# Gated attention and feed-forward block: query path by tokens with DMA turns, matrix integers on GpSimd, one set of loads for three head groups

## The chip, the cores and the metric

One core of one Trainium2 chip. The metric is the time of the whole kernel on the device in microseconds (us), smaller being better; three runs before gave 962.68 to 965.32 us, median 962.88.

## What is computed

Activations x of shape (4, 512, 512) in float32 go through four gated residual steps; the context is (4, 512, 512). The changed part lies between the second and the third.

```python
x = x + tanh(g_xattn[0]) * wkv(w, u, layernorm(x), ctx)       # a recurrence over 512 positions
n = layernorm(x)
h = silu(bitlinear(n, w1)) * bitlinear(n, w2)                 # activations to 8 bits by groups of 64
x = x + tanh(g_ffn[0]) * bitlinear(h, w3)                     # weights are signs times a mean
n = layernorm(x)
q = qdq(n) @ qdq(wq).T + bq      # qdq: scale of a row = max|.| / 127, round, clip to 127
k, v = split(ctx @ wkv.T + bkv)
o = softmax(q k^T / sqrt(32)) v                               # 16 heads of 32
x = x + tanh(g_xattn[1]) * (qdq(o) @ qdq(wp).T + bp)
x = x + tanh(g_ffn[1]) * (quantised rmsnorm(x) @ ternary(W).T)
```

## The kernel before

The program is written engine by engine: SyncE (all DMAs), GpSimd, ScalarE, TensorE and VectorE each have one list of instructions in order, and semaphores join them. Nothing is planned by a tool; the order on each engine is the order of the code. X, all 2048 tokens, stays in SBUF as 16 token tiles of 128.

**Stages.** Set-up and recurrence end at about 191 us. Then comes the feed-forward stage, one token tile after another (i = 0 to 15), each in four slots (j = 0 to 3) of 512 hidden columns. In a slot TensorE makes the two up products of tile i (`up`, line 1098: 16 matmuls, halves of fp16 high and low parts) and the down product of tile i - 1 (`down`, line 1110: 8 matmuls). VectorE takes the pair to a quantised hidden block: `hidden` (lines 1516 to 1521), after ScalarE's rounding `scaled` (1527). ScalarE writes the fp16 high part (811), GpSimd the low part (594), and SyncE turns the block by a DMA transpose (`turn_h`, 419). `up` of slot c waits until `scaled` of slot c - 2 is done. Between these lie the preparation of the tile to come (`prep_...`; 1425 to 1436) and two passengers:

- the **query path**, a few tiles behind: statistics (1540), normalising (831), maximum and scale (1548 to 1550), rounding (835), integers (1555). Then `q_turn` (1119, 1121) turns the integers on TensorE, and multiplies ones by a diagonal matrix of the token scales, which GpSimd made (606), to have them along columns; ScalarE copies both out (841, 842); `q_project` (1132) makes 16 matmuls of 128 columns, the result with channels on the partitions; VectorE multiplies the scales in (`q_full`, 1560), ScalarE applies channel scale and bias in four pieces (848) and the high part (852), GpSimd the low part (612). All queries stand in `QALL`, channels on partitions.
- the **matrices** wq, W and wp: for each VectorE takes row maxima (1568), ScalarE rounds (818), VectorE makes the integers (1587; 1589 and 1590 for the ternary one), SyncE turns four blocks (461). `matrix_work` (lines 328 to 331) says in which slot: maxima in tiles 1 and 7, integers one slot late from tiles 2, 5 and 8; the mean of W at tile 4 (1578).

**Seam.** After the last up part SyncE loads keys, values and queries of batch 0 from DRAM and `QALL` into `KS`, `VB` and `QS`, which lie where the up weights lay: for each of four head groups 3 + 1 + 12 DMAs (426, 429, 438), two groups, then the offsets, then the two others. TensorE meanwhile finishes the last down parts and query tiles 12 to 15; `first_rows` are the score rows of group 0.

**Attention.** 16 groups (4 batches of 4 head groups), 16 slots each. In a slot TensorE makes about one score row for the group to come (`rows`, 1161), whose maximum VectorE takes (1642), and a score tile of this group (`scores`, 1180), ScalarE its exponential (936); `weigh` (1190) multiplies with the values. GpSimd adds the weights, eight additions a group (`add_weights`, 663). The maxima are turned (`c_turn`, 1169), split into a high part (909) and a low part (1650) and sent as two rows into `QS` (`send_c`, 447); the first `scores` of a group waits for them. Then comes the output stage.

Of the kernel before, what the change touches and what calls it, by code (L numbers as in the profile page):

```python
# [5 lines left out]
F32 = mybir.dt.float32  # L6
# [54 lines left out]
def flamingo_kernel(nc, x, ctx_2048, g_xattn, g_ffn, w, u, w1, w2, w3, wq, bq, wkv, bkv, wp, bp, gamma, wl, out):  # L61
    stack = ExitStack()
    with stack:
# [29 lines left out]
        W_, U_, BQ, BK = vec[:, 0:4], vec[:, 4:8], vec[:, 8:12], vec[:, 12:16]  # L93
# [4 lines left out]
        vrows = sb("vrows", [4 * DB, P], F32)  # L98
# [67 lines left out]
        at = used[0]  # L166

# [6 lines left out]
        SXB, DIAG = part(P, F32), part(P, F32)  # L174
        QF, QB = part(D, F32, "p (k t) -> p k t", k=DB), part(D, F32, "p (k t) -> p k t", k=DB)
# [4 lines left out]
        wm_ints = B[:, used[0]:used[0] + DB * D].rearrange("p (k d) -> p k d", k=DB)  # L180
        OT, SM = part(512, F32), part(512, F32)
# [18 lines left out]
        swp_dram = nc.dram_tensor("swp_row", (D,), F32, kind="Internal").ap()  # L200
# [42 lines left out]
        st3, rstd3, qs3, rnd3, li3, diag3 = sem("st3"), sem("rstd3"), sem("qs3"), sem("rnd3"), sem("li3"), sem("diag3")  # L243
        lt_out, sx_ps, qp_ps, qb_ready = sem("lt_out"), sem("sx_ps"), sem("qp_ps"), sem("qb_ready")
# [15 lines left out]
        NSMALL = 6  # L260
# [76 lines left out]
        def _(sp):  # L337
            for to, frm in ((vrows[0:4, :], by_block(w)), (vrows[4:8, :], by_block(u)), (vrows[8:12, :], by_block(bq)),
                            (vrows[12:16, :], by_block(bkv[0:D])),
                            (TG[:, 0:2], on_all(g_xattn, 2)), (TG[:, 2:4], on_all(g_ffn, 2))):  # L340
                sp.dma_start(to, frm).then_inc(small_in, 16)
# [90 lines left out]
            def load_q(b, g):  # L432
                if g == 0:
                    sp.wait_ge(q_hi, b * TB + TB)
                    sp.wait_ge(q_lo, b * TB + TB)
# [22 lines left out]
            def turn_block(m, k):  # L458

                sp.wait_ge(wm_ready, DB * m + k + 1)  # L460
                sp.dma_start_transpose((WQT, WLT, WPT)[m][:, :, k * P:k * P + P], wm_ints[:, k, :]).then_inc(wm_out, 16)

            load_matrix(0)
            sp.wait_ge(ff_scales, 1)
            for i in range(TOK):
                for j in range(FC):
                    turn_h(i, j)
                    for m, k in matrix_work(i, j, INTS):
                        turn_block(m, k)
                        if k == DB - 1 and m < 2:  # L470
                            load_matrix(m + 1)
                    if (i, j) == (INTS[2] + 1, 1):
                        sp.dma_start(swp_dram.rearrange("(k p) -> p k", p=P), SWQP[:, 4:8],
                                     allow_slow_non_contiguous=True).then_inc(swp_io, 16)
                    if (i, j) == (INTS[2] + 3, 1):
                        sp.wait_ge(swp_io, 16)
# [1335 lines left out]
```

## Time and profile before

| | us |
|---|---|
| median of three runs | 962.88 (962.68 to 965.32) |
| profiled execution, its own time | 966.35 |
| its span from first to last instruction | 964.6 |
| TensorE busy | 821.9 |
| VectorE busy | 759.5 |
| ScalarE busy | 576.9 |
| GpSimd busy | 487.2 |
| set-up and recurrence | 0 to 191 |
| feed-forward stage, up parts | 191 to 555 |
| seam | 555 to 594 |
| attention | 594 to 864 |
| output stage | 864 to 965 |

PE is TensorE (PEld its weight loads), DVE VectorE, ACT ScalarE, POOL GpSimd, SPq SyncE's queue. Matmuls overlap, so their start-to-start distance is the time that they hold the engine; a row for several shows the time from the first start to the last end. Starts are in us from the start of the span. In brackets stands the idle time before, and what ended it. Spans on GpSimd are rough.

### The profile page before, as it was taken

The page shows a single profiled execution, that of the slowest core. Times are in us where ns is not written, and L with a number is a line of the kernel's source. Part 1 is how long each engine was busy: PE and PEld are TensorE (multiplying, and loading weights), DVE is VectorE, ACT ScalarE, POOL GpSimd, SP SyncE. Part 2 cuts the span into 40 slices and gives each one's busy share as a digit, 9 for nine tenths or more (in the row PEclk, how much of TensorE's full clock was granted, in tenths as well). Part 3 has the DMA queues.
Part 4 walks back from the last instruction along what each step waited for, and adds up shares of the span by engine and source line. Part 5 has one row for each costly group of instructions (what it writes and reads, how often), then busy time and mean ns, then how long its engine had stood idle before and what let it go on. Part 6 is the DMA issues. An engine that isn't in the chain of part 4 may idle for free.

```text
span 964.6 us, 14534 instructions
## 1 busy us (share of the span) xinstructions
PE 821.9 (85%) x4373; PEld 353.2 (37%) x4373; DVE 759.5 (79%) x1510; ACT 576.9 (60%) x974; POOL 487.2 (51%) x560
## 2 busy tenths in 40 slices
PE   2899987789898989899999968799999999974754
PEld 2544443334344444444444432222223232222321
DVE  4699998879899899999998758477777777634884
ACT  3588886543555565666665544466666666655762
POOL 2866663223334444444444343475757575764761
PEclk9999999899999999999999986899999999996886
DMA  8668875533353442352433241212122221000111
GB/s 283 214 178 221 223 204 151 143 88 65 62 115 55 72 103 57 63 70 55 79 65 65 45 100 54 84 49 79 55 77 57 72 61 46 1 1 0 43 66 66
DMA packets 172392, 86.51 MB, mean 90 GB/s; under 512 B 124048, under 2 KB 156960, under 8 KB 172320
## 3 DMA queue, kind: packets, MB, share of 16 engines
q1 hardware_dynamic: 172320, 85.64, 35.6%
q8 instruction: 34, 0.56, 0.2%
q14 instruction: 38, 0.31, 0.1%
HBM read 37.76 MB, written 12.58 MB: 52 GB/s over the span
## 4 chain that ended last, share of the span: by engine, by line
PE 37%; DVE 22%; issue 7%; ACT 6%; SPq 4%; DMA 3%; POOL 0%; ACTq 0%; DVEq 0%
PE bank L1098 10%; PE bank L1190 5%; PE bank L1161 5%; PE bank L1110 4%; PE bank L1180 4%; DMA A<-B 3%; DVE bank L1516 3%; DVE gsm L1518 3%; DVE B L1527 2%; SPq L438 2%; DVE B L1521 2%; PE bank L1307 2%; ACT bank L806 2%; PE bank L1209 2%; PE bank L1199 2%
## 5 line engine op out<-in xcount | busy, mean ns | idle before, releaser
L1098 PE MATMUL bank<-A,B 128*128 128x512 f16 x1024 | 233.0, 381 | 15.8 <-DVE B L1527 15.6
L1642 DVE TENSOR_REDUCE B<-bank 128x1 f32<-128x512 f32 x256 | 168.0, 683 | 73.9 <-PE bank L1161 73.9
L936 ACT ACTIVATE A<-bank 128x512 f32<-128x512 f32 x256 | 144.1, 593 | 106.9 <-PE bank L1180 103.5
L594 POOL TENSOR_TENSOR B<-B 128x512 f16<-128x512 f32 x64 | 76.4, 1193 | 223.4 <-DVE B L1527 147.2
L1098 PEld LDWEIGHTS bank<-A,B 128*128 128x128 f16 x1024 | 98.8, 98 | 142.9 <-DVE B L1527 20.6
L663 POOL TENSOR_TENSOR B<-A 128x512 f32<-128x512 f32 x64 | 79.3, 1269 | 96.0 <-ACT A L936 96.0
L806 ACT ACTIVATE bank<-B 128x512 f32<-128x512 f32 x64 | 38.5, 602 | 137.4 <-DVE B L1521 137.4
L1110 PE MATMUL bank<-A,B 128*128 128x512 f16 x512 | 120.7, 379 | 0.0
L1180 PE MATMUL bank<-A 98*128 98x512 f16 x256 | 94.5, 390 | 21.2 <-ACT A L936 10.5
L1161 PE MATMUL bank<-A 96*128 96x512 f16 x256 | 97.7, 409 | 7.9 <-DMA A<-B 4.7
L663 POOL TENSOR_TENSOR B<-B,A 128x512 f32<-128x512 f32 x64 | 79.0, 1264 | 0.1
L1190 PE MATMUL bank<-A,B 128*32 128x512 f32 x512 | 69.6, 616 | 1.0 <-ACT A L936 1.0
L1110 PEld LDWEIGHTS bank<-A,B 128*128 128x128 f16 x512 | 49.5, 98 | 54.3 <-DMA B<-B 0.4
L1073 PE MATMUL bank<-B 128*128 128x512 f16 x192 | 47.2, 399 | 17.9 <-DVE B L1411 17.9
L1527 DVE SCALAR_TENSOR_TENSOR B<-bank,gsm 128x512 f32<-128x512 f32 x64 | 44.2, 691 | 16.1 <-ACT bank L806 14.0
L1516 DVE SCALAR_TENSOR_TENSOR bank<-bank,ffs,B 128x512 f32<-128x512 f32 x64 | 48.2, 753 | 9.1 <-PE bank L1098 8.6
L1161 PEld LDWEIGHTS bank<-A 96*128 96x128 f16 x256 | 23.3, 100 | 85.0 <-DVE B L1642 65.3
L801 ACT ACTIVATE B<-bank,ffs 128x512 f32<-128x512 f32 x64 | 43.1, 673 | 13.4 <-PE bank L1098 13.1
L549 POOL TENSOR_SCALAR B<-X,mv,rs 128x128 f32<-128x128 f32 x64 | 49.8, 792 | 0.4
L1180 PEld LDWEIGHTS bank<-A 98*128 98x128 f16 x256 | 25.0, 99 | 67.2 <-ACT A L936 36.6
L1062 PE MATMUL bank<-B 128*128 128x512 f16 x192 | 46.1, 392 | 0.0
L1518 DVE TENSOR_REDUCE gsm<-bank 128x8 f32<-128x512 f32 x64 | 44.3, 692 | 2.2
(216 smaller groups left out, 1479.5 us busy)
## 6 DMA issues: line engine op xcount, KB each, us to landing
B<-in_L_ffn_w_dram SPq DMA_DIRECT2D x48, 256.0 KB, 3.4
A<-k_parts SPq DMA_DIRECT2D x48, 128.0 KB, 2.6
A<-B SPq DMA_DIRECT2D x192, 32.0 KB, 1.9
X<-in_x_dram SPq DMA_DIRECT2D x4, 1024.0 KB, 9.4
B<-in_ctx_dram SPq DMA_DIRECT2D x16, 256.0 KB, 4.4
k_parts<-B SPq DMA_DIRECT2D x16, 256.0 KB, 4.3
v_rows<-B SPq DMA_DIRECT2D x16, 256.0 KB, 2.3
B<-v_rows SPq DMA_DIRECT2D x16, 256.0 KB, 3.4
```

The costliest lines, as they stand in the source:

```text
L594: nc.gpsimd.tensor_tensor(HLb[j][:, 1, :], Db[j % 2], HLb[j][:, 0, :], ALU.subtract).then_inc(lo_done, 1)
L663: nc.gpsimd.tensor_tensor(ACC[j], PR[j] if t == 1 else ACC[j], PR[(HG * t + j) % 8], ALU.add).then_inc(acc_done, 1)
L936: nc.scalar.activation(PR[(HG * t + j) % 8], bank[2 + j % 2][:, :], ACT.Exp, scale=SCALE).then_inc(exp_done, 1)
L1098: last = mm(bank[2 * n + q][:, :], XQT[a][:, m, :], wt[:, m % DB, j * 512:j * 512 + 512], start=(m == 0), stop=(m == 2 * DB - 1))
L1110: last = mm(bank[5 + q][:, :], HT[j][:, m, :], W3T[:, DB * j + m % DB, :], start=(j == 0 and m == 0), stop=(j == FC - 1 and m == 2 * DB - 1))
L1161: mm(bank[ROW_BANKS[r % 3]][:, :], QS[0:96, HG * g + j, t * P:t * P + P], KS[0:96, HG * g + j, :], start=True, stop=True).then_inc(row_ps, 1)
L1180: mm(bank[2 + j % 2][:, :], KS[0:98, HG * g + j, t * P:t * P + P], QS[0:98, HG * g + j, :], start=True, stop=True).then_inc(st_ps, 1)
L1190: last_ = mm(bank[6][DH * j:DH * j + DH, :], VB[:, t, (HG * g + j) * DH:(HG * g + j + 1) * DH], PR[(HG * t + j) % 8], start=(t == 0), stop ...
L1516: stt(H, H, C2, SAb[q], ALU.mult, ALU.mult).then_inc(h_done, 1)
L1518: link(reduce(gsm[:, 0, :], grouped(H), AX.X, ALU.max, apply_absolute_value=True))
L1527: stt(grouped(Db[q]), grouped(bank[q][:, :]), RND, spread(1), ALU.subtract, ALU.mult).then_inc(d_done, 1)
L1642: reduce(NMX[g % 2][:, t, j:j + 1], bank[ROW_BANKS[r % 3]][:, :], AX.X, ALU.max, negate=True).then_inc(row_max, 1)
```

## The change

- Query integers are turned by a DMA transpose (`turn_ints`); `q_turn` and the diagonal matrix go. `q_project` makes four matmuls of 512 columns with tokens on the partitions, one slot earlier. ScalarE scales out of PSUM by token (`q_scale`), GpSimd multiplies the channel scales and adds the bias (`q_affine`, two operations of full width), ScalarE and GpSimd make the two parts, and a second DMA transpose puts them into `QALL` (`turn_q`). `q_full` and `q_bias` go.
- The matrices' integers are made on GpSimd, in two buffers.
- The mean of W is taken at the second slot of tile 4, not at its last.
- One scale of the activation groups reads 1024 from a per-partition operand instead of an immediate.
- Channel scales of wq and wp go through DRAM to a row on all partitions; the query bias is loaded over the value bias.
- At the seam group 0 is loaded alone, the other three groups by one set of 3 + 1 + 12 larger DMAs. Query tiles 13 to 15 are finished during the score rows and inside attention; the last one's turn stands ahead of the offsets of group 2.

```diff
@@ SyncE
+            def turn_ints(u):
+                sp.wait_ge(li3, u + 1)
+                up_to(sp, qp_ps, u)
+                sp.dma_start_transpose(LT, LI).then_inc(lt_in, 16)
+
+            def turn_q(u):
+                sp.wait_ge(q_hi, u + 1)
+                sp.wait_ge(q_lo, u + 1)
+                sp.dma_start_transpose(QALL[:, :, :, u * P:u * P + P].rearrange("p h k s -> p (h k) s"),
+                                       QHL[u % 2].rearrange("p h d -> p (h d)")).then_inc(qT_in[u % 2], 16)
...
+                    if j == 0 and i > 4:
+                        turn_q(i - 5)
+                    if j == 1 and i > 2:
+                        turn_ints(i - 3)
...
-            for g in range(2):
-                load_kv(0, g, True)
-                load_q(0, g)
+            def load_others():
+                for slot, part_ in ((0, 0), (1, 0), (2, 1)):
+                    ins = sp.dma_start(KS[DH * slot:DH * slot + DH, HG:HEADS, :],
+                                       k_dram[0][part_, P:D, :].rearrange("(j p) s -> p j s", p=DH))
+                    ins.then_inc(kv_in[1], 16)
+                sp.dma_start(VB[:, :, P:D], v_dram[0].rearrange("(t p) d -> p t d", p=P)[:, :, P:D]).then_inc(kv_in[1], 16)
+                for slot, part_ in ((0, 0), (1, 1), (2, 0)):
+                    for j in range(HG):
+                        sp.dma_start(QS[DH * slot:DH * slot + DH, HG + j:HEADS:HG, :],
+                                     QALL[DH * j:DH * j + DH, part_, 1:DB, 0:SEQ]).then_inc(q_in[1], 16)
+            turn_ints(TOK - 3)
+            turn_q(TOK - 5)
+            load_kv(0, 0, True)
+            load_q(0, 0)
+            turn_ints(TOK - 2)
+            turn_q(TOK - 4)
+            load_others()
             send_c(0, 0)
-            for g in range(2, DB):
-                load_kv(0, g, True)
-                load_q(0, g)
+            turn_q(TOK - 3)
+            turn_ints(TOK - 1)
+            turn_q(TOK - 2)
...
+                    if first and g == 1:
+                        turn_q(TOK - 1)
+                        scales_in(1)
                     if not (last and g == DB - 1):
                         send_c(*following(b, g))
@@ GpSimd
+            def q_affine(u):
+                pool.wait_ge(qf_ready, u + 1)
...
+                step.link(nc.gpsimd.tensor_tensor(QF(u), QF(u), swp_all[:, :], ALU.mult))
+                nc.gpsimd.tensor_tensor(QF(u), QF(u), bv_all[:, :], ALU.add).then_inc(qb_ready, 1)
...
+            def ints_block(m, k):
+                n = DB * m + k
+                pool.wait_ge(wm_round, ROUNDED(m, k))
+                up_to(pool, wm_out, 16 * n)
+                raw, ints = wm_raw[:, k, :], wm_ints[k % 2]
+                if m != 1:
+                    nc.gpsimd.tensor_scalar(ints, raw, RND, 127.0, ALU.subtract, ALU.min).then_inc(wm_ready, 1)
+                else:
+                    step.link(nc.gpsimd.tensor_scalar(raw, raw, RND, -1.0, ALU.subtract, ALU.max))
+                    nc.gpsimd.tensor_scalar(ints, raw, 1.0, None, ALU.min).then_inc(wm_ready, 1)
...
-                        if j == 0 and there(i - 3):
-                            q_diag(i - 3)
+                        if j == 0 and there(i - 4):
+                            q_affine(i - 4)
...
-                        if j == 2 and there(i - 4):
+                        if j == 3 and there(i - 4):
                             q_low(i - 4)
                         lo_part(i, j)
+                        for m, b in matrix_work(i, j, INTS):
+                            ints_block(m, b)
...
+                    if first and g == 0:
+                        q_affine(TOK - 1)
+                    if first and g == 1:
+                        q_low(TOK - 1)
@@ ScalarE
+            def q_scale(u):
+                act.wait_ge(qp_ps, u + 1)
...
+                nc.scalar.activation(QF(u), bank[7][:, :], ACT.Copy, scale=QSC[:, u % 4:u % 4 + 1]).then_inc(qf_ready, 1)
@@ TensorE
             def q_project(u):
-                pe.wait_ge(lt_out, u + 1)
+                pe.wait_ge(lt_in, 16 * (u + 1))
...
                 for k in range(DB):
-                    for j in range(DB):
-                        last_ = mm(bank[7][:, k * P:k * P + P], WQT[:, j, k * P:k * P + P], LT[:, j, :],
-                                   start=(j == 0), stop=(j == DB - 1))
+                    last_ = mm(bank[7][:, :], LT[:, k, :], WQT[:, k, :], start=(k == 0), stop=(k == DB - 1))
...
-                        if j == 0 and there(i - 4):
-                            q_project(i - 4)
-                        if j == 2 and there(i - 3):
-                            q_turn(i - 3)
+                        if j == 3 and there(i - 3):
+                            q_project(i - 3)
...
             down(TOK - 1, 0, 1)
             down(TOK - 1, 1, 1)
-            q_turn(TOK - 3)
+            q_project(TOK - 3)
             down(TOK - 1, 2, 1)
             down(TOK - 1, 3, 1)
...
+            first_rows(0, 16)
...
             c_turn(0, 0)
+            q_project(TOK - 2)
...
+                        if slot == 4 and opening:
+                            q_project(TOK - 1)
@@ VectorE
-                ts(gsm[:, 7, :], gsm[:, 5, :], XUP, None, ALU.mult)
+                ts(gsm[:, 7, :], gsm[:, 5, :], eps[:, 4:5], None, ALU.mult)
...
-                        if j == 0 and there(i - 4):
-                            q_full(i - 4)
...
-                            elif b == FC - 1:
+                            elif b == 1:
                                 mean_scale()
-                        for m, b in matrix_work(i, j, INTS):
-                            ints_block(m, b)
...
-            first_maxima(0, 2)
-            q_full(TOK - 2)
-            q_ints(TOK - 1)
-            first_maxima(2, 8)
-            q_full(TOK - 1)
-            first_maxima(8, 16)
+            first_maxima(0, 16)
             maxima(0, 1, 0)
             c_low(0, 0)
+            q_ints(TOK - 1)
```

## Rows read from the trace of the kernel before

**Rows 1.** Busy time by stretch, tile 11: length, PE, PEld, DVE, ACT, POOL, clock, DMA.

```profile
445.90:468.00 22.10, 22.10 (x119) 10.78 (x118) 20.44 (x46) 13.98 (x26) 10.35 (x17) 1.00 0.36 71
```

**Rows 2.** Timeline of TensorE, tile 10: start, us, operation.

```profile
427.23 1.06 PE L1132 MATMUL bank<-B,WQT 128*128 128x128 f16 x16
428.12 1.89 PE L1110 MATMUL bank<-A,B 128*128 128x512 f16 x8
429.85 3.62 PE L1098 MATMUL bank<-A,B 128*128 128x512 f16 x16
...
438.48 0.39 PE L1119 MATMUL bank<-id,B 128*128 128x128 f16 x4
...
438.98 1.89 PE L1110 MATMUL bank<-A,B 128*128 128x512 f16 x8
```

**Rows 3.** VectorE: L1418 once a tile (tiles 1, 10, 11); groups by line and shape.

```profile
220.32 0.69 DVE L1418 BATCH_NORM_STATS2 st<-X 128x6 f32<-128x512 f32 x1
...
434.23 0.69 DVE L1418 BATCH_NORM_STATS2 st<-X 128x6 f32<-128x512 f32 x1
...
455.74 0.69 DVE L1418 BATCH_NORM_STATS2 st<-X 128x6 f32<-128x512 f32 x1
...
L1560 DVE TENSOR_TENSOR B<-bank,B 128x512 f32<-128x512 f32 x16 | 11.0, 685 | 2.0 <-PE bank L1132 2.0
```

**Rows 4.** Timelines of VectorE and GpSimd, where one operation outlasts its usual time.

```profile
396.23 1.05 DVE L1519 TENSOR_SCALAR gsm<-gsm,ffs 128x8 f32<-128x8 f32 x1
...
396.10 1.15 POOL L612 TENSOR_TENSOR B<-B 128x512 f16<-128x512 f32 x1
...
238.00 1.38 DVE L1508 TENSOR_TENSOR bp_all<-bp_all,vec 128x512 f32<-128x512 f32 x1
```

**Rows 5.** Groups of VectorE: the matrices' integers; busy, mean ns, idle before.

```profile
L1587 DVE TENSOR_SCALAR B<-B 128x512 f16<-128x512 f32 x8 | 6.4, 801 | 1.8 <-ACT B L818 1.8
...
L1589 DVE TENSOR_SCALAR B<-B 128x512 f32<-128x512 f32 x4 | 3.0, 758 | 0.8 <-ACT B L818 0.8
L1590 DVE TENSOR_SCALAR B<-B 128x512 f16<-128x512 f32 x4 | 2.6, 656 | 0.1
```

**Rows 6.** Groups of GpSimd: the one large tensor_scalar that it has.

```profile
L549 POOL TENSOR_SCALAR B<-X,mv,rs 128x128 f32<-128x128 f32 x64 | 49.8, 792 | 0.4
```

**Rows 7.** Timeline of SyncE's queue, and the DMA list (median us to landing).

```profile
409.17 1.27 SPq L461 DMA_TRANSPOSE WPT<-B  x1
...
442.04 17.25 SPq L419 DMA_TRANSPOSE B<-B  x4
...
564.40 8.16 SPq L438 DMA_DIRECT2D A<-B  x12
...
WQT<-B SPq DMA_TRANSPOSE x4, 2.5
```

**Rows 8.** Timelines of TensorE and VectorE, seam and first groups of attention.

```profile
573.98 1.44 PE L1161 MATMUL bank<-A 96*128 96x512 f16 x3 [4.67 <-DMA A<-B]
...
593.58 0.61 PE L1180 MATMUL bank<-A 98*128 98x512 f16 x1
...
603.30 0.38 PE L1161 MATMUL bank<-A 96*128 96x512 f16 x1 [1.47 <-issue]
...
614.84 0.61 PE L1180 MATMUL bank<-A 98*128 98x512 f16 x1 [4.49 <-DMA A<-B]
...
583.24 4.86 DVE L1642 TENSOR_REDUCE B<-bank 128x1 f32<-128x512 f32 x8
```

**Rows 9.** Busy time by stretch: after the wait at 614.84, and group 2 whole.

```profile
615.00:622.00 7.00, 7.00 (x29) 1.14 (x31) 2.40 (x4) 1.79 (x3) 0.00 (x0) 0.58 0.33 97
634.09:650.52 16.43, 15.38 (x93) 4.64 (x94) 11.90 (x20) 10.30 (x20) 11.07 (x10) 1.00 0.23 65
```

**Rows 10.** Timelines of GpSimd and SyncE, end of group 2.

```profile
645.64 4.95 POOL L663 TENSOR_TENSOR B<-B,A 128x512 f32<-128x512 f32 x4
...
648.00 1.32 SPq L447 DMA_DIRECT2D A<-B  x2
```

More of the change, by code:

```diff
@@ L179, in flamingo_kernel @@
         CT = [part(512, F16) for _ in range(2)]
-        wm_ints = B[:, used[0]:used[0] + DB * D].rearrange("p (k d) -> p k d", k=DB)
-        OT, SM = part(512, F32), part(512, F32)
+        wm_ints = [B[:, used[0] + D * n:used[0] + D * n + D] for n in range(2)]
+        OT = part(512, F32)
+        QHL = [B[:, used[0]:used[0] + 2 * D].rearrange("p (h d) -> p h d", h=2), QHL_1]
+        SM = part(512, F32)
+        QF = lambda u: QF_1 if u < TOK - 1 else QF_LAST
         RDEN = part(16, F32)
@@ L433, in load_q @@
                 if g == 0:
-                    sp.wait_ge(q_hi, b * TB + TB)
-                    sp.wait_ge(q_lo, b * TB + TB)
+                    for n in range(2):
+                        sp.wait_ge(qT_in[n], 16 * TB // 2 * (b + 1))
                 for slot, part_ in ((0, 0), (1, 1), (2, 0)):
@@ L868, in tiles @@
                             prep_hi(i + 1)
-                        if j == 1 and there(i - 4):
-                            q_bias(i - 4)
+                        if j == 0 and there(i - 4):
+                            q_scale(i - 4)
+                        if j == 2 and there(i - 4):
+                            q_high(i - 4)
                         if j == 2 and not last:
@@ L874, in tiles @@
                             q_norm(i - 2)
-                        if j == 3 and there(i - 3):
-                            q_operands(i - 3)
                         round_up(c, j % 2)
@@ L919, in sums_out @@
                 act.wait_ge(sum_ps, n + 1)
+                if isinstance(n, int) and n == 0:
+                    act.wait_ge(qT_in[0], 16 * TOK // 2)
                 up_to(act, s_ps, n)
@@ L941, in attend @@
                                 sums_out(*preceding(b, g))
+                            if opening and (t, j) == (0, 3):
+                                q_high(TOK - 2)
+                            if opening and (t, j) == (1, 1):
+                                q_scale(TOK - 1)
+                            if first and g == 1 and (t, j) == (1, 0):
+                                q_high(TOK - 1)
                             if (t, j) == (2, 2) and not closing:
@@ L1112, in down @@
                 last.then_inc(down_ps, 1)
-            def q_turn(u):
-                pe.wait_ge(li3, u + 1)
-                up_to(pe, lt_out, u)
-                for k in range(DB):
-                    turn(bank16[4][:, k * P:k * P + P], LI[:, k * P:k * P + P], id16[:, :])
-                pe.wait_ge(diag3, u + 1)
-                mm(bank[4][:, D // 2:D // 2 + P], ones[:, :], DIAG, start=True, stop=True).then_inc(sx_ps, 1)
             def q_project(u):
-                pe.wait_ge(lt_out, u + 1)
+                pe.wait_ge(lt_in, 16 * (u + 1))
                 up_to(pe, qf_ready, u)
@@ L1157, in rows @@
                 if n == 0:
[L1158 to L1159 removed]
+                    if b == 0 and g > 0:
+                        pe.wait_ge(kv_in[1], 64)
+                        pe.wait_ge(q_in[1], 192)
+                    else:
+                        pe.wait_ge(kv_in[g], (b if g > 1 else b + 1) * 64)
+                        pe.wait_ge(q_in[g], (b if g > 1 else b + 1) * 192)
                 up_to(pe, row_max, r - 2)
```

156 lines of the change are left out of this document (63 added, 93 removed).

## The prediction

> **What bounds it now.** I read the busy time by stretch first, then the timelines of TensorE, VectorE, SyncE and GpSimd. In a late feed-forward tile TensorE is busy for all of its 22.10 us at full clock, VectorE for 20.44 [rows 1]. TensorE's own rows give the same period: 8 matmuls take 1.73 us start to start (0.216 each), so 96 take 20.73; the query projection holds it 0.89 and the query turn 0.50, together 22.12 [rows 2]. VectorE is barely faster. From tile 10 to 11 its own period is 21.51, and it is still working off a lag [rows 3]. In tiles 1 to 9 it sets the pace: from the first of those rows to the second are nine tiles in 213.9 us, 23.8 each, because it scales the three matrices and makes their integers there. So the stage has two nearly equal bounds, and what leaves TensorE counts fully only in the last six tiles.
>
> The seam is bound by SyncE: twelve query loads take 8.16 us to issue [rows 7], and the first score rows wait for the last (4.67 us) [rows 8]. Group 0 is then held 1.47 us and the start of group 1 by 4.49 us by loads and by the offsets queued behind them [rows 8].
>
> **The change, part by part.**
>
> TensorE per tile: projection and turn (0.89 + 0.50) go, four 512-column matmuls come, 4 x 0.216 = 0.86. That is 22.12 - 21.59 = 0.53 saved, over the last six tiles 3.2 us.
>
> VectorE loses the 12 blocks of integers: 8 x 0.80 + 4 x (0.76 + 0.66) = 12.1 us, the 2.6 us that it stood before them for ScalarE [rows 5], and about 1 us of small scales that they had pushed into a GpSimd operation. It also loses about 1.0 us of waiting around the matrix mean, which now comes two slots earlier. Sum -16.7.
>
> What comes back is contention. A VectorE scale of 8 elements, of the form that has a per-partition scalar, took 1.05 us, ending where a GpSimd subtraction of 1.15 us ended; and a VectorE product of two SBUF operands took 1.38 us [rows 4], against 0.69 for the same size [rows 3]. The Trainium skill, SBUF — State Buffer, section "Who interferes with whom", states that GpSimd and a two-port or two-input VectorE operation lock each other out for a whole instruction; by that rule the trace agrees. So each block of integers on GpSimd, which follows ScalarE's copy and GpSimd's own low part (1.15) and so starts some 2.6 us after the slot's last product, delays the next small scale, due 3 to 4 us after it. How much depends on a duration that no row shows: tensor_scalar, 128x512, on GpSimd. Below it is bounded by half of the two-input row, 0.6; above by four times the 128-element tensor_scalar, 4 x 0.79 = 3.2 [rows 6]. I take 1.2, near the 512-element row (1.15) [rows 4], the nearest in size. Then four blocks of an ordinary matrix cost 1.85 us (nothing in the slot whose small scale comes latest) and those of the middle one, two operations each, 2.55: +6.2. The skill's GPSIMD Engine Reference, section 3.1, gives 769 ns for one 512-element loop; by that the blocks would cost about 3 us and the total would be 3 lower. No run here shows it.
>
> Query path: the 0.69 us product leaves VectorE [rows 3]; on GpSimd two products of full width come, 2.4 us, placed where VectorE quantises the next activations with two SBUF operands: 0.56 of delay. Net -0.1 a tile, -0.6 over tiles 4 to 9. ScalarE loses four 128-column operations and two copies, gains one of full width, and has room. Giving one small scale a per-partition scalar gains nothing by my reading, since the 1.05 us row has one [rows 4]; at most 0.8 a tile.
>
> The turn by DMA: SyncE issues two more transposes a tile, 1.27 us each [rows 7], with room. But TensorE now waits for one. SyncE turns the hidden block of slot 1 from 442.04, so the integers' turn follows at 443.3 and lands 2.5 us later [rows 7], at 445.8. TensorE starts the up part of slot 3 at 438.98 + 1.73 = 440.7 and is done 16 x 0.216 = 3.46 later, at 444.2 [rows 2]: it would wait 1.6 us, with a down part and the next tile's up parts queued behind. As long as VectorE lags, this time is VectorE's anyway. Where TensorE takes over, its start moves from 3.46 to 5.8 us after VectorE's last product in slot 1 (2.0 for the low part, 1.27 and 2.5 for the turns): 2.3 once. As a loop (projection 0.86, down part 1.73, up part 3.46, down and up 5.18, VectorE's block, at most a quarter of 20.44 and taken as 4.0, then 5.8 to the landed turn) it is 21.0 us a tile, just under 21.6, so it does not bind again. Plus 0.8 for uneven slots, as VectorE's margin shrinks from 0.6 to 0.1. The first turns of the matrices now wait on GpSimd in SyncE's queue, a microsecond or two ahead of the next hidden turn, which is needed a tile later: nothing. The row of biases loaded again, three more rows of scales (0.6 each to issue), the smaller set-up transpose and the low part moved to slot 3 cost nothing, in SyncE's and GpSimd's idle time. Feed-forward in all: -16.7 + 6.2 - 0.6 - 3.2 + 2.3 + 0.8 = -11.2.
>
> Seam: two transposes are issued ahead of the first loads, 2 x 1.27 = +2.5, so rows start at 576.5. Sixteen rows now run with no projection or turn between them at VectorE's 0.61 each [rows 8], to 586.7, and c_turn ends near 588. The next row needs the one set of loads for three groups. SyncE issues two turns and 16 loads after 575.1, ending at 587.7 if a larger load costs the same 0.63 to issue; they land near 590. Row and maximum 1.1, low part 0.7, sending 1.3 and landing with the start 1.6 add 4.7: scores start near 594.8 against 593.58, +1.2. The bound below is 0 and above +5, if 3 MB land slower. TensorE pays the last projection inside group 0, 0.9 to 1.7 (take 1.3). The late projection of token tile 13 stalls the down parts by some 3 us before the loads land; those loads are its cover.
>
> Gone are 1.47 and 4.49 - 0.4 of waits, and the slow clock behind the second: the granted clock is 0.58 in the 7 us after it, mostly the 1.2 GHz level after an idle engine, and that group takes 614.84 to 634.09, 19.25 us, against 16.43 [rows 8, 9]: 2.8. Together -8.4.
>
> What is late next: the last query tile. SyncE's turn of it waits for GpSimd's low part, which is put behind all eight sums of group 1. GpSimd ends those sums at 650.59, at the very end of a group, while the offsets are already sent from 648.00 [rows 10]. Queued behind the turn are the row of scales and the offsets of group 2. After the group's end come 1.16 (low part) + 1.27 + 0.6 + 1.32 + 1.2 (landing) = 5.6 us, 5.3 more than now, and the same 2.8 of slow clock: +8.1. Seam and attention: 1.2 + 1.3 - 8.4 + 8.1 = +2.2. The output stage is untouched; its scales are loaded long before.
>
> **Sum.** -11.2 + 2.2 = -9.0. The profiled execution took 966.35 us (span 964.6), so 957.3; it is 3.5 above the median of the runs, 962.88, which puts the median at 953.9, given as 954.
>
> **Rivals.** A change under 0.3% (2.9 us) is about what a measurement cannot tell from none.
>
> (1) As worked out: 954, own range 949 to 959. Chance 0.45.
>
> (2) Less contention, or a load set and last turn that are not late: GpSimd's operation at 0.6 gives 3.5 back, a per-partition scalar that escapes the lock up to 5, an unhindered group 2 another 8. For it: VectorE reached its scales before GpSimd in most slots. Time about 944. Chance 0.20.
>
> (3) Slower: GpSimd's integers take 2.5 us. Then the twelve blocks, sixteen operations, hold VectorE's small scales some 1 to 1.3 us longer an operation, and low parts queue behind the double ones (1.15 + 5 in a slot of 5.4); the cost is about 23 instead of 6.2, the time 954 + 17 = 971. It decides from some 1.9 us an operation, where the 9 us are used up. For it: 0.79 us for 128 elements [rows 6], and very small GpSimd operations far shorter, so that time may go by elements. Against: that row has two per-partition scalars. Chance 0.17.
>
> (4) The DMA turn binds every tile: if landing or SyncE is 1.6 us later than in the rows, the 21.0 loop becomes 22.6, and six late tiles lose 1.0 each, seven before them 0.4: 963. For it: one queue carries all turns. Chance 0.18.
>
> **Numbers.** Predicted is (1), 954. With (2)'s 944 and (4) inside, 943 to 966 leaves out the worse half of (3) and a tail below. Faster by over 0.3% (under 960): 0.45 + 0.20 + a part of (4) 0.05 = 0.70. Same 0.14, mostly (4). Slower 0.16.
>
> **What would show it.** Late tiles of 21.6 us with a VectorE period of about 21.5; GpSimd tensor_scalar near 1.2 us; small scales over 0.5 us behind each; matmuls of L1132's successor hardly waiting for a DMA; first rows 2.5 us later after the last up part; 4.49 gone and a wait of 5 to 6 us for a DMA at the first scores of group 2. Wrong if late tiles exceed 22, if GpSimd's operation is over 1.9, or if group 2 starts unhindered.

## The result and the profile after

The changed kernel takes **1006.52 us** (median of 4 runs, 1005.7 to 1008.39), the kernel before 964.1 in the same session (4 runs): a ratio of 1.0439, 95% interval 1.0409 to 1.047. That is 42 us slower. I had predicted 954 and a range of 943 to 966. The profiled execution took 1005.91 us, its span is 1004.0, its mean granted clock 0.928 against 0.955.

The page of the changed kernel: its engines' sums, then its groups, with busy time, mean ns of one, and idle time before them with its releaser.

```profile
PE 826.7 (82%) x4085; PEld 340.7 (34%) x4085; DVE 754.8 (75%) x1478; ACT 547.9 (55%) x894; POOL 548.0 (55%) x576
...
L1577 DVE SCALAR_TENSOR_TENSOR bank<-bank,ffs,B 128x512 f32<-128x512 f32 x64 | 48.3, 754 | 45.2 <-PE bank L1172 44.9
...
L1197 PE MATMUL bank<-WQT,B 128*128 128x512 f16 x64 | 22.3, 484 | 43.7 <-DMA B<-B 43.6
```

TensorE has 5 us more of busy time and VectorE 5 less; GpSimd's 61 more are still only 55% of the span. The extra span is idle time. One row owns most of it: L1197, the query projection, waits 43.6 us for "DMA B<-B", the turned integers (39.4 of them before the last up part). VectorE in turn waits 44.9 us for TensorE (8.6 before). The timeline of TensorE, line L1197 alone, shows where (the last column is the wait before it):

```profile
282.78 1.89 PE L1197 MATMUL bank<-WQT,B 128*128 128x512 f16 x4 [8.91 <-DMA B<-B]
...
334.27 1.54 PE L1197 MATMUL bank<-WQT,B 128*128 128x512 f16 x4 [4.41 <-DMA B<-B]
365.57 1.89 PE L1197 MATMUL bank<-WQT,B 128*128 128x512 f16 x4 [7.86 <-DMA B<-B]
...
416.15 1.50 PE L1197 MATMUL bank<-WQT,B 128*128 128x512 f16 x4 [4.09 <-DMA B<-B]
447.48 1.89 PE L1197 MATMUL bank<-WQT,B 128*128 128x512 f16 x4 [7.89 <-DMA B<-B]
471.85 1.04 PE L1197 MATMUL bank<-WQT,B 128*128 128x512 f16 x4 [1.04 <-DMA B<-B]
494.92 1.04 PE L1197 MATMUL bank<-WQT,B 128*128 128x512 f16 x4 [1.31 <-DMA B<-B]
```

These are tiles 3, 5, 6, 8, 9, 10 and 11. Two readings: every tile up to 12 waits at least a microsecond, and the tiles in which a matrix is turned or loaded wait 4 to 9. The duration tells of the clock: four matmuls take 1.04 us after a short wait and 1.89 after a long one. The stretches that hold the long waits (columns: stretch, length, PE, PEld, DVE, ACT, POOL busy, granted clock, DMA share, GB/s) have a lower granted clock than the one without:

```profile
255.00:290.00 35.00, 25.34 (x108) 10.55 (x107) 25.02 (x54) 13.23 (x23) 13.96 (x17) 0.85 0.48 98
...
452.00:583.00 131.00, 127.27 (x588) 56.88 (x586) 112.59 (x230) 65.71 (x109) 65.05 (x85) 1.00 0.42 75
```

The account by stage, from the two timelines of TensorE (us; the moment at which each stage is over, and its difference in the last column):

| | before | after | lost in this stage |
|---|---|---|---|
| last up part ends | 554.9 | 583.3 | 28.4 |
| first scores | 593.58 [rows 8] | 628.47 | 6.5 |
| first scores of group 2 | 634.09 [rows 9] | 667.69 | -1.3 |
| first scores of group 3 | 650.52 | 686.36 | 2.2 |
| first product of the output stage | 872.12 | 908.09 | 0.1 |
| end of the span | 964.6 | 1004.0 | 3.4 |

The differences add up to the 39.4 us between the two spans. The medians are 42.4 apart, mostly because the profiled execution before took 966.35 us, 2.2 above its median. Of the 28.4 us of the feed-forward stage, 27.1 are waits of TensorE: 45.2 us (39.4 for the turned integers, 5.8 for VectorE) where it had 18.1.

In attention the two waits forecast as gone are gone, and the one forecast as new is there, where SyncE's turn of the last query tile follows GpSimd's low part (TensorE's row, then GpSimd's, then SyncE's):

```profile
667.69 0.61 PE L1246 MATMUL bank<-A 98*128 98x512 f16 x1 [6.11 <-DMA A<-B]
...
661.52 1.15 POOL L669 TENSOR_TENSOR B<-B 128x512 f16<-128x512 f32 x1
...
662.74 1.28 SPq L478 DMA_TRANSPOSE B<-B  x1
664.06 0.58 SPq L490 DMA_DIRECT2D swp_all<-scale_rows  x1
664.74 0.69 SPq L451 DMA_DIRECT2D A<-B  x1
```

### The profile page after: what moved, and what is told of

It is laid out like the page before. It is cut to its first block, busy times and chain, and to the rows that moved or that the text cites. A ratio compares the mean times of both kernels' runs of the same rounds, so it can differ in the third digit from the quotient of the medians.

```text
span 1004.0 us, 13854 instructions
## 1 busy us (share of the span) xinstructions
PE 826.7 (82%) x4085; PEld 340.7 (34%) x4085; DVE 754.8 (75%) x1478; ACT 547.9 (55%) x894; POOL 548.0 (55%) x576
## 4 chain that ended last, share of the span: by engine, by line
PE 34%; DVE 19%; issue 9%; DMA 6%; SPq 5%; ACT 4%; POOL 4%; ACTq 0%; DVEq 0%; POOLq 0%
PE bank L1172 6%; PE bank L1227 5%; PE bank L1256 5%; PE bank L1246 4%; PE bank L1184 4%; DMA B<-B 3%; DMA A<-B 2%; DVE bank L1577 2%; PE bank L1368 2%; DVE gsm L1579 2%; DVE B L1588 2%; PE bank L1197 2%; DVE gsm L1580 2%; PE bank L1277 2%; PE bank L1265 2%
## 5 line engine op out<-in xcount | busy, mean ns | idle before, releaser
L1172 PE MATMUL bank<-A,B 128*128 128x512 f16 x1024 | 233.9, 382 | 6.0 <-DVE B L1588 5.8
L649 POOL TENSOR_TENSOR B<-B 128x512 f16<-128x512 f32 x64 | 76.0, 1188 | 185.8 <-DVE B L1588 92.1
L1172 PEld LDWEIGHTS bank<-A,B 128*128 128x128 f16 x1024 | 100.1, 98 | 130.9 <-DVE B L1588 9.5
L1184 PE MATMUL bank<-A,B 128*128 128x512 f16 x512 | 127.0, 394 | 0.0
L880 ACT ACTIVATE bank<-B 128x512 f32<-128x512 f32 x64 | 38.5, 601 | 156.8 <-DVE B L1582 156.8
L1577 DVE SCALAR_TENSOR_TENSOR bank<-bank,ffs,B 128x512 f32<-128x512 f32 x64 | 48.3, 754 | 45.2 <-PE bank L1172 44.9
L1184 PEld LDWEIGHTS bank<-A,B 128*128 128x128 f16 x512 | 52.1, 102 | 66.9 <-issue 11.9
L1147 PE MATMUL bank<-B 128*128 128x512 f16 x192 | 47.9, 403 | 17.8 <-DVE B L1472 17.8
L1197 PE MATMUL bank<-WQT,B 128*128 128x512 f16 x64 | 22.3, 484 | 43.7 <-DMA B<-B 43.6
L635 POOL TENSOR_TENSOR B<-B 128x512 f16<-128x512 f32 x16 | 18.9, 1182 | 49.7 <-ACT B L854 40.3
```

The source lines that it names most:

```text
L649: nc.gpsimd.tensor_tensor(HLb[j][:, 1, :], Db[j % 2], HLb[j][:, 0, :], ALU.subtract).then_inc(lo_done, 1)
L1172: last = mm(bank[2 * n + q][:, :], XQT[a][:, m, :], wt[:, m % DB, j * 512:j * 512 + 512], start=(m == 0), stop=(m == 2 * DB - 1))
L1184: last = mm(bank[5 + q][:, :], HT[j][:, m, :], W3T[:, DB * j + m % DB, :], start=(j == 0 and m == 0), stop=(j == FC - 1 and m == 2 * DB - 1))
L1577: stt(H, H, C2, SAb[q], ALU.mult, ALU.mult).then_inc(h_done, 1)
```

## The experiments

My theory after the result (T): the feed-forward stage lost its time to the projection's wait for the DMA turn, not to the busy engines. Its rival (C): the contention of GpSimd's matrix integers with VectorE, rival 3 of the prediction. GpSimd's `tensor_scalar` did take 1.92 us, the point from which that rival was to decide. Twelve kernels were run; each time is a median, to be held against the kernel before in the same session (964.3 to 965.2).

**1. The turn ahead of the transfers in SyncE's queue.**

```
                    for m, k in matrix_work(i, j, INTS):
                        turn_block(m, k)
-                       if k == DB - 1 and m < 2:
-                           load_matrix(m + 1)
+                   if j == 1 and i > 2:
+                       turn_ints(i - 3)
+                   for m in range(2):
+                       if (i, j) == (INTS[m] + 1, 1):
+                           load_matrix(m + 1)
...
-                   if j == 1 and i > 2:
-                       turn_ints(i - 3)
```

> Theory T: the changed kernel lost its 42 us in the feed-forward stage because TensorE waits in slot 3 for a projection operand that is turned by DMA on SyncE's one queue. Three of its waits (8.9, 7.9 and 7.9 us, token tiles 3, 6 and 9) stand behind a 1 MB matrix load or the 4-byte scale column that SyncE issued just ahead of that turn. With the turn issued ahead of them these three become like their neighbours, 1 to 4 us: 16 to 20 us of waits and some 6 us of slow clock behind them go, time 980 to 986, and the two waits of 4 us in tiles 5 and 8 stay. Rival C (GpSimd's integers hold VectorE, as in rival 3 of the prediction): the order of transfers changes little, 1000 or more.

Measured 991.3 us, ratio 1.0277 (1.0233 to 1.032): 15 us back, less than T said, more than C. The three long waits became 6.96, 4.38 and 1.88. So only the third, behind the scale column, was due to the transfer ahead of it as I had read it; the other two lost 2.0 and 3.5 us by the edit. What is left of them has a second cause: SyncE stands for GpSimd, which is late by the matrix integers (SyncE's row of tile 3, then GpSimd's).

```profile
272.76 1.19 SPq L465 DMA_TRANSPOSE WQT<-B  x1
274.06 1.24 SPq L391 DMA_TRANSPOSE B<-B  x1
276.45 1.23 SPq L423 DMA_TRANSPOSE B<-B  x1
277.74 1.27 SPq L472 DMA_TRANSPOSE B<-B  x1
...
270.82 1.92 POOL L679 TENSOR_SCALAR B<-B 128x512 f16<-128x512 f32 x1 [2.31 <-DMA WQT<-B]
...
275.24 1.16 POOL L650 TENSOR_TENSOR B<-B 128x512 f16<-128x512 f32 x1
```

The last matrix block is turned at 272.76, and behind it the next activations, the hidden block and, fourth, the integers for which TensorE waits. GpSimd first stood 2.31 us for the turn of the block before, since its `ints_block` waits for that turn, and ended the block at 272.74; so its low part of the hidden block came late too, until 276.40, and SyncE turns that block at 276.45.

**2. The projection one slot later.** It moves from slot 3 to slot 0 of the next tile; ScalarE's and GpSimd's scaling follow it. The mean of W goes back to the last slot of tile 4, where the kernel before has it; this holds for all runs built on this one.

```
-                       if j == 3 and there(i - 3):
-                           q_project(i - 3)
+                       if j == 0 and there(i - 4):
+                           q_project(i - 4)
```

> The projection of a token tile moves from slot 3 to slot 0 of the next tile, one slot (5.4 us) behind the same turn; all other work stays. Theory T: nearly all 39 us of waits in the stage go and the slow clock behind them, and what I forecast for the stage (11 us less than before) can show; with the 11 us that seam, attention and output lost in the changed kernel, 962 to 970. Waits of 3 us may stay in tiles 3, 6 and 9. Rival C: 1000 or more, since the contention is as it was.

Measured 983.22 us, 1.019 (1.0156 to 1.0225): 23 us back, where T said 36 to 44. The one-microsecond waits are gone, the group's wait fell from 43.6 to 9.9, of which 5.2 are for the turn of tile 9, behind the scale column. But two waits of 5.80 and 6.66 us turned up at the up parts (L1172), which need the next activations. Their turn is queued on SyncE behind the matrix load too; the projection's own wait, which came first in the changed kernel, had covered that. In run 3, which puts the load behind the turns, TensorE waits for no DMA at its up parts (L1173 there); in run 5 2.95 us of such a wait come back.

**3. Both edits.**

> Turn issued first and projection one slot later together. Theory T: as the late projection alone, or up to 5 us below it, where its waits in tiles 3, 6 and 9 still show: 960 to 968. Rival C: 1000 or more.

Measured 970.51 us, 1.0071 (1.0048 to 1.0093): 36 of the 42 us back, 2.5 short of T's range. The last up part now ends at 549.7, 5.2 before the kernel before. One stall of this kernel comes with the later scaling: in tile 6 ScalarE stands 9.03 us for GpSimd's scaled row, which comes behind two matrix blocks, and TensorE 4.67.

```profile
349.20 0.62 ACT L922 CAST B<-B 128x512 f16<-128x512 f32 x1 [9.03 <-POOL B L666]
...
351.05 0.69 DVE L1590 SCALAR_TENSOR_TENSOR B<-bank,gsm 128x512 f32<-128x512 f32 x1 [7.99 <-ACT bank L881]
...
351.89 6.07 PE L1173 MATMUL bank<-A,B 128*128 128x512 f16 x16 [4.67 <-DVE B L1590]
```

**4. The matrices' integers back on VectorE,** in the changed kernel, all else as it was.

The first two lines leave GpSimd's loop, the last two come in VectorE's, with the block's function.

```
                        lo_part(i, j)
-                       for m, b in matrix_work(i, j, INTS):
-                           ints_block(m, b)
...
                                mean_scale()
+                       for m, b in matrix_work(i, j, INTS):
+                           ints_block(m, b)
```

> The changed kernel with the twelve blocks of matrix integers back on VectorE, in the same slots, each waiting for the turn of the block before it as on GpSimd. Theory T: the long waits for the turn stay, those of 4 us in tiles 5 and 8 shrink to about 1 (SyncE no longer waits for GpSimd), 6 us less, and VectorE gets back 12 us of work, part of which lies beside TensorE's waits: 1000 to 1008. Rival C: the contention is gone, worth some 23 us of VectorE's time against 12 given back: 985 to 995.

Measured 1001.64 us, 1.0369 (1.0324 to 1.0414). Rival C falls: undoing its cause gives 5 us, not 12 to 22, and the last up part still ends at 582.5; in the traces 2.8 of the 4.0 us won lie in the output stage (run 12). The waits of tiles 3, 5 and 6 shrank, from 8.91, 4.41 and 7.86 to 4.77, 2.91 and 2.23; the 8.67 behind the scale column stayed. But TensorE waits 14.1 us for VectorE in this stage in exchange, 5.8 in the changed kernel, and a TensorE that comes later to a turn waits less for it. Counted from the projection of the tile before, those of tiles 5 and 6 come 1.5 and 2.7 us earlier than in the changed kernel; that of tile 3 comes 1.5 later, counted from the up part at 243. So this run shows 1.5 and 2.7 us that SyncE stood for GpSimd's integers, and nothing for tile 3.

**5. ScalarE's high half at the end of its slot** (on top of 3). `q_high(i - 4)` moves from ahead of `round_up` to behind `high(i, j)` in slot 2.

> Both edits of the run before, and ScalarE's high half of the query row goes from the start of slot 2 to its end. There ScalarE stood 9.0 us in token tile 6 for GpSimd's scaled row, which came behind two blocks of matrix integers, and the activation of the slot was queued behind it; VectorE stood 8.0 us, TensorE 4.7. Theory: 4.7 us of TensorE and about 2 us of slow clock go, 963 to 967. Rival: the wait only moves on to the next instruction of the same tile, 969 to 972.

Measured 966.42 us, 1.0031 (1.0016 to 1.0047): as expected, and the last up part ends at 545.8. The wait of 4.67 us became one of 2.95, for a DMA.

**6. The last query turn behind the offsets** (on top of 5).

```
-                   if first and g == 1:
-                       turn_q(TOK - 1)
-                       scales_in(1)
                    if not (last and g == DB - 1):
                        send_c(*following(b, g))
+                   if first and g == 1:
+                       turn_q(TOK - 1)
+                       scales_in(1)
```

> The run above, with the turn of the last query tile and the row of scales put behind the offsets of group 2 in SyncE's queue, not ahead of them. If the 6.0 us wait of the first scores of group 2 is SyncE's wait for GpSimd's eight sums, it goes with the 2.3 us of slow clock behind it: 8.3 us below the run above, and that group takes 16.4 us. Rival: the offsets would have been late by themselves or by the loads ahead of them, under 3 us.

Measured 959.9 us, 0.9961 (0.9941 to 0.998), 6.5 below the run above where 8.3 were expected. In the traces from the first scores to those of group 3 it is 48.90 us against 56.09, so 7.2; the wait at group 2 is 0.41. Here the last up part ends at 543.6. **This is the stage end that I had forecast, 554.93 - 11.2 = 543.7**, but in part by luck: in this kernel the 2.3 us for the turn are not paid, the mean of W has its old place (TensorE stands 3.45 us for it), and a wait of 2.79 us for a DMA in tile 6 was in no term.

**7. Two sets of loads** (on top of 6): group 1 by itself, one set for groups 2 and 3 after the offsets (`load_others` is cut to these two).

```
-           load_others()
+           load_kv(0, 1, True)
+           load_q(0, 1)
            send_c(0, 0)
            turn_q(TOK - 3)
            turn_ints(TOK - 1)
+           load_others()
            turn_q(TOK - 2)
```

> The run above, with the first loads of group 1 by themselves (16 loads, 32 KB each for queries) and one set for groups 2 and 3 sent after the offsets of group 0. Theory: the first scores wait for the landing of the large set (8.3 us from issue for 96 KB against 1.9 for 32 KB), so they come 4 to 5 us earlier and nothing later waits: 4 to 5 us below the run above. Rival: the set for groups 2 and 3 lands too late for the rows of group 2 or holds the offsets of group 1 in the queue, and the gain is given back: within 1 us of the run above.

Measured 962.1 us, 0.9983 (0.9969 to 0.9997), 2.2 above run 6: the rival's mechanism, at more than the 1 us that it had. The first scores do come 4.9 us earlier, counted from the last up part (40.7 against 45.6), but TensorE stands 4.42 us in group 0 for the set of groups 2 and 3, and group 2 begins 3.1 us later than in run 6, counted in the same way.

**8. The kernel before, with only the matrices' integers on GpSimd.** The block of four buffers and the turn by TensorE stay.

```
                        lo_part(i, j)
+                       for m, b in matrix_work(i, j, INTS):
+                           ints_block(m, b)
...
-                       for m, b in matrix_work(i, j, INTS):
-                           ints_block(m, b)
```

> The kernel before, with only the twelve blocks of matrix integers moved from VectorE to GpSimd: this has no turn by DMA that TensorE waits for. By the terms of my sum (15.7 us off VectorE, 6.2 of contention back) it is 9.5 us faster than before: 953 to 957. Rival C (a 1.9 us operation on GpSimd holds VectorE's small scales, the point from which rival 3 decides): no gain or slower, 963 to 970. Between them, 958 to 962, the contention is larger than my term and smaller than rival 3.

Measured **953.74 us**, 0.9888 (0.9868 to 0.9908): 10.6 us faster, where 9.5 were expected, and that with the long operation in it (GpSimd's integers, then VectorE's small scale between 250 and 540 us, last the same scale in the kernel before):

```profile
L621 POOL TENSOR_SCALAR B<-B 128x512 f16<-128x512 f32 x8 | 15.4, 1920 | 0.7
L623 POOL TENSOR_SCALAR B<-B 128x512 f32<-128x512 f32 x4 | 7.7, 1930 | 0.0
L624 POOL TENSOR_SCALAR B<-B 128x512 f16<-128x512 f32 x4 | 6.0, 1504 | 0.3
...
L1533 DVE TENSOR_SCALAR gsm<-gsm,ffs 128x8 f32<-128x8 f32 x53 | 15.9, 300 | 1.9
...
L1519 DVE TENSOR_SCALAR gsm<-gsm,ffs 128x8 f32<-128x8 f32 x51 | 13.5, 264 | 1.8
```

With four buffers GpSimd waits for no turn between the blocks of one matrix here. The last up part ends at 542.7.

**9. and 10. One part of the seam on top of run 8:** the one set for groups 1 to 3 right after the loads of group 0 (9), or two sets (10), with TensorE's old query path. `load_rest` is the changed kernel's `load_others`.

```
-           for g in range(2):
-               load_kv(0, g, True)
-               load_q(0, g)
-           send_c(0, 0)
-           for g in range(2, DB):
-               load_kv(0, g, True)
-               load_q(0, g)
+           load_kv(0, 0, True)
+           load_q(0, 0)
+           load_rest()
+           send_c(0, 0)
```

> The kernel before with GpSimd's matrix integers (the last run of the former set, 953.7) and, of the seam's edits, the one set of loads for groups 1 to 3 alone; no query turn by DMA. Theory: group 1's wait of 4.3 us and 2.5 us of slow clock behind it go; the set lands some 8 us after its last issue, so the first scores come 1 to 3 us later: 947 to 950. Rival: the set of 96 KB loads costs at the first scores what it gives at group 1: 952 to 955.

> As the run above but group 1 keeps its own loads and groups 2 and 3 share one set behind the offsets of group 0. SyncE then has 16 loads ahead of the offsets of group 1, not 32: the 4.3 us wait and its slow clock go, and the rows of group 2, which TensorE wants from slot 8 of group 0, wait 1 to 3 us for the set: 946 to 950. Rival: those rows wait as long as the offsets did: 952 to 955.

Measured **946.65 us**, 0.9805 (0.9784 to 0.9826), and 950.52 us, 0.986 (0.9836 to 0.9884). The single set takes 7 us off run 8 and makes the fastest kernel of the study. Its first scores come as soon after the last up part as in run 8 (38.9 us against 38.5): TensorE still has projections to make among the first rows, and behind them the set lands unnoticed. In run 10 the rows of group 2 wait 3.0 us for the smaller set, and what is won is 3.2. SyncE's queue of run 9, the first loads, the set, and the next entry:

```profile
552.78 8.49 SPq L438 DMA_DIRECT2D A<-B  x12
561.31 1.60 SPq L484 DMA_DIRECT2D A<-k_parts  x3
562.96 0.47 SPq L486 DMA_DIRECT2D B<-v_rows  x1
563.47 7.89 SPq L489 DMA_DIRECT2D A<-B  x12
579.64 15.73 SPq L447 DMA_DIRECT2D A<-B  x4
```

**11. The turns of query tiles 11 to 14 behind all first loads** (on top of 7), since only later batches read them.

> The run f3 (the changed kernel with late projection, turns first, last turn behind the offsets, two sets of loads) with the turns of query tiles 11 to 14, which only later batches read, put behind all the first loads. Theory: rows and first scores come 2.5 us earlier and the set for groups 2 and 3 some 1.3 to 5 us earlier: 953 to 958. Rival: GpSimd and ScalarE, which wait for those turns before they reuse the buffer, hold the first exponentials, and it is 960 or more.

Measured 974.72 us, 1.0096 (1.0074 to 1.0118), a miss. The rival's chain is in ScalarE's timeline: it stands 19.43 us in front of the high half of tile 13, whose buffer waits for the turn of tile 11, and the exponentials of group 0 are queued behind it.

```profile
599.71 0.62 ACT L922 CAST B<-B 128x512 f16<-128x512 f32 x1 [19.43 <-DMA B<-B]
...
602.87 0.61 PE L1247 MATMUL bank<-A 98*128 98x512 f16 x1 [14.88 <-ACT A L1003]
```

**12. Sixteen instructions without use on VectorE** (on top of 6), for the 3.4 us of the output stage, which the change does not touch. There one operation of VectorE takes 2.83 us where its like take 0.69; it is shown in the last section.

```
+           for n in range(16):
+               link(nc.vector.memset(held[:, 3:4], 0.0))
            for k in range(TOK // 2):
```

> The run f2 (959.9 median) with sixteen one-column memsets more on VectorE at the start of the feed-forward stage, about 1 us in all. In every version of the changed kernel with its instructions on VectorE as they were, the output stage has one 1024-column tensor_scalar of 2.83 us in place of 0.69, where VectorE stood 0.27 us for nothing the profile names just before it and GpSimd's 2.4 us product started first; with 16 more VectorE instructions (integers back on VectorE) it is not there. Theory: that stop sits at a fixed count of VectorE's instructions; moved on by 16, it meets no such collision, the long operation is gone and the output stage takes 93 to 94 us in place of 96; time 957 to 959. Rival: the collision comes from when the output stage starts against GpSimd or from the row of scales, and stays: 960 to 961, one operation of 2.8 us as before.

Measured 955.8 us, 0.9911 (0.9892 to 0.9931): 4.1 below run 6, a little more than expected. The long operation is gone, and the output stage takes 92.8 us in place of 96.0 in the traces.

## Why the prediction was wrong

**The failed step is the DMA turn of the integers on SyncE's queue,** priced at 2.3 us once, with the sentence that a loop of 21.0 us "does not bind again". It bound in every tile from 3 to 12: 39.4 us of waits before the last up part, and slow clock behind the long ones. Three things were wrong in it.

First, the loop itself. Its tail was right: in tile 11 VectorE's product of slot 1 ends at 489.05, and TensorE projects at 494.92, 5.9 later where I had 5.8. The block of VectorE ahead of it I took as 4.0 us. From the end of slot 1's up part (483.09) to 489.05 it is 5.96. VectorE begins 1.4 us after the up part, because it comes late from the slot before, where one of its small scales took 1.31 us beside GpSimd's new 128x512 products (VectorE's rows, then GpSimd's):

```profile
479.63 1.31 DVE L1580 TENSOR_SCALAR gsm<-gsm,ffs 128x8 f32<-128x8 f32 x1
...
486.00 0.73 DVE L1580 TENSOR_SCALAR gsm<-gsm,ffs 128x8 f32<-128x8 f32 x1
...
479.65 1.27 POOL L664 TENSOR_TENSOR B<-B,swp_all 128x512 f32<-128x512 f32 x1 [0.78 <-ACT B L916]
480.99 1.27 POOL L665 TENSOR_TENSOR B<-B,bv_all 128x512 f32<-128x512 f32 x1
```

With 5.96 and 5.9 the loop is 23.1, and so is the time from the projection's end at 472.73 to the next at 495.79. Tiles 13 and 14, in which nothing waits, take 21.75. That the turn binds every tile was rival (4), which I priced at 963 from a loop of 22.6, with landing or SyncE 1.6 us late. Landing and SyncE were as forecast in this tile; it was VectorE's block that was 2.0 longer.

Second, the queue. I wrote that the matrices' turns, waiting on GpSimd in SyncE's queue, cost nothing, because the next hidden turn was needed a tile later. But the integers' turn stands in the same queue and is needed at once. Run 4 shows this for 1.5 and 2.7 us in tiles 5 and 6. In tile 3 it shows none, since with the integers on VectorE the hidden block itself came late; there run 1's rows show SyncE standing for the matrix block, and then for the low part that came late behind it.

Third, what lies ahead in that queue. The matrix loads and the scale column were there before, and the sum listed none of them because they cost nothing there. They became dear when TensorE began to wait for a transfer behind them: run 1 takes 2.0, 3.5 and 6.0 us off the three long waits by order alone. SyncE's row shows it for the column (0.58 us to issue) and the turn that follows it; TensorE starts on that turn's data at 447.48, 7.9 us after 439.59:

```profile
438.59 0.58 SPq L484 DMA_DIRECT2D scale_rows<-vec  x1
439.59 1.23 SPq L472 DMA_TRANSPOSE B<-B  x1
```

**The sum of the other terms came out, its contention term did not.** Integers off VectorE against contention: 9.5 us forecast for this part by itself, run 8 gives 10.6 (964.31 to 953.74). GpSimd's operation was 1.92 and 1.50 us, not 1.2, yet the cost followed neither my term of 6.2 nor rival 3: in run 8 VectorE's small scale takes 300 ns on average where it took 264 (53 and 51 of them between 250 and 540 us), 2 us in all. Each of the twelve blocks does run beside one small scale, but that scale then takes 0.23 to 0.58 us (once 1.01, beside a low part too), and 0.23 by itself. So the point from which rival 3 was to decide was reached, and its price per operation was far too high, and mine as well. The query path, where I had put 0.56 a tile, holds the same scale more: in run 6, which has both, it averages 407 ns over the whole stage against 280 before, 8 us in all, though operations of GpSimd that the change had only shifted are among those beside it. The Trainium skill's GPSIMD Engine Reference, section 3.1, gives 769 ns for a loop over 512 elements; this operation took 2.5 times as long, so that estimate was no guide here. The whole stage of run 6 ended at 543.6 against 543.7, with the reservations made there.

The scalar operand given to one small scale gained nothing, as said: L1489 has a median of 895 ns, its counterpart in the kernel before 899.

**Seam.** The first rows came 21.4 us after the last up part, 21.6 forecast. The first scores came 45.1 after it where I had 39.9. The step that was short: "land near 590", 2.3 us after the last issue. Issue ended 33.9 us after the last up part (32.8 forecast), and the rows start at 623.89, 6.7 us after it. The page has 8.3 us to landing for the 96 KB loads against 1.9 for the 32 KB ones. I had a bound of +5 for this and +6.5 came. Run 7, with smaller sets, has its first scores 4.9 us earlier. In run 9 the same set costs 0.4 us, since its SyncE issues it straight after group 0's loads and TensorE has work until it lands. In the changed kernel two transposes stand ahead of it and TensorE has none.

**Attention.** Right. From first scores to those of group 3: 56.94 before, 57.89 after, +0.95; my terms for it (+1.3 - 8.4 + 8.1) give +1.0. The new wait of 6.11 us was forecast as 5.6, and run 6 shows its cause: with the turn behind the offsets it is 0.41.

**Output stage.** Said to be untouched, and 3.4 us longer; a step that I did not have, next section.

## What to carry to other kernels

When an operand is moved from an engine to a DMA queue, list everything that stands ahead of it in that queue at each turn of the loop, with the waits of those entries and the landing of large or scattered transfers. What is harmless in a queue on which nobody waits becomes a stall of the bound engine once it waits there. Take a change of several parts apart before keeping it: here one part alone (integers on GpSimd) gave 10.6 us and another on top (one set of loads) 7.1; with the query turn by DMA and its order in the queue, the kernel stood 42 above the start. And when a loop time is worked out against a bound with 3% between them, its least certain block must be read from the trace, not taken as a share.

## What was new of the hardware

**A one-input operation held for 2.1 us by a start 0.12 us too late.** In the output stage VectorE takes the integers of 1024 columns in 0.69 us. In one case it took 2.83, where GpSimd's 2.41 us product of two SBUF operands began first (VectorE's rows, then GpSimd's):

```profile
946.38 0.69 DVE L1798 TENSOR_SCALAR B<-B 128x1024 f16<-128x1024 f32 x1 [0.27 <-issue]
946.99 2.83 DVE L1764 TENSOR_SCALAR B<-B 128x1024 f16<-128x1024 f32 x1
...
946.87 2.41 POOL L754 TENSOR_TENSOR B<-B,swp_all 128x1024 f32<-128x1024 f32 x1
```

In the other steps VectorE's operation starts first and GpSimd only follows. It is late here by the 0.27 us in which it stood for nothing that the profile names. The long operation is in every run of the changed kernel that has as many VectorE instructions as it (after, runs 1, 2, 3, 5, 6, 7, 11), and in neither run that has 16 more of them (4 and 12). In those with it the stop stands at the same instruction of the stage, though they come to it at times from 898 to 946 us. This points to a place in VectorE's instruction stream, and not to the time or the data; what it is stays open. The output stage takes 94.1 to 96.0 us with the long operation and 92.4 to 94.7 without. The operation is 2.1 us of the 3.4 that the stage lost; what makes up the rest was not traced. The Trainium skill, SBUF — State Buffer, section "Who interferes with whom", says that a `tensor_scalar` can take the shared port pair and that whoever issues first keeps it for the whole instruction; the trace agrees.

**Entries of one queue delay one another well beyond their issue.** The transpose of the next activations, 1.28 us to issue in the median, took 4.14 two entries behind a 1 MB matrix load (tile 6). The integers' turn, 2.5 us to landing in the median, took up to 7.8; in tile 9, where it stands one entry behind the 2 KB scale column, TensorE starts on it 7.9 us after its issue. The column itself takes 8.5 us to landing, for 512 elements of 4 bytes.

**A long wait costs more than itself.** After the wait of 8.91 us the four matmuls of the projection take 1.89 us at a granted clock of 0.50 (from 283 to 285 us), which is the 1.2 GHz level, and the eight of the down part behind it 2.93 from start to start, where they take 1.73 at full clock; then the full level is back.

```profile
284.46 3.09 PE L1184 MATMUL bank<-A,B 128*128 128x512 f16 x8
287.39 3.62 PE L1172 MATMUL bank<-A,B 128*128 128x512 f16 x16
```
